# First layers and Haar attention of a one-core hybrid network kernel: steps regrouped over the engines

## The reference

```python
q = l2_normalize(apply_rope(x @ W_Q, cos, sin))      # rotation of two halves of 32
k = l2_normalize(apply_rope(x @ pinv(W_Q).T, cos, sin))
v = x @ W_V.T
attn_coef = (W_h.T q)(W_h.T k).T * scale             # W_h: Haar basis, constant over blocks of 32 tokens
attn = where(near, q k.T * scale, W_h attn_coef W_h.T)   # near only the own token with these masks
attn = attn / sqrt(number of visible tokens)          # causal
attn = softmax((attn - mean) / std) over visible tokens
y = attn @ v @ W_O.T
```

## Time and profile before

| | us |
|---|---|
| three runs | 367.94, 369.97, 475.1 |
| median of the three | 369.97 |
| profiled execution | 368.61 |
| its span, first to last instruction | 366.8 |
| of it: first layers, up to the attention's first steps | 0 to 45 |
| multi-head attention | 45 to 183.5 |
| first mixture and its layer norm | 183.5 to 231 |
| layer norm and Haar attention | 231 to 263.1 |
| layer norm, gate | 263.1 to 275.4 |
| second mixture | 275.4 to 366.8 |

### The profile page before, as it was taken

How to read it: one execution, slowest core, us unless ns; L and a number is a source line. 1 busy time by engine, 2 the same in 40 slices (tenths; PEclk the granted TensorE clock), 3 DMA queues, 4 the chain that set the end, 5 groups by cost and what they waited for, 6 DMA issues and landing times.

```text
span 366.8 us, 6880 instructions
## 1 busy us (share of the span) xinstructions
PE 333.8 (91%) x2287; PEld 214.7 (59%) x2296; DVE 265.8 (72%) x682; ACT 220.2 (60%) x557; POOL 164.0 (45%) x177
## 2 busy tenths in 40 slices
PE   8885669999999999999889999968698999999996
PEld 5652346777776777666464333524456776666661
DVE  2888898888889888887572786897986844445650
ACT  1554478889898888889539553542144643344550
POOL 6000057655556565555300000040200999999994
PEclk9998778999999999999989999988999999999999
DMA  7934000000000000000000992000003966656521
GB/s 214 249 110 152 0 1 0 3 3 1 2 0 3 3 0 2 2 2 0 2 3 8 334 386 82 2 1 0 2 2 113 348 194 217 209 199 207 173 81 58
DMA packets 16275, 30.86 MB, mean 84 GB/s; under 512 B 5808, under 2 KB 9584, under 8 KB 16240
## 3 DMA queue, kind: packets, MB, share of 16 engines
q1 hardware_dynamic: 15776, 29.60, 24.9%
q10 hardware_dynamic: 464, 0.82, 0.9%
HBM read 29.70 MB, written 0.72 MB: 83 GB/s over the span
## 4 chain that ended last, share of the span: by engine, by line
PE 68%; DVE 16%; ACT 8%; issue 4%; DMA 1%; POOL 1%; SPq 0%; DVEq 0%; ACTq 0%; POOLq 0%
PE ps L1148 15%; PE ps L1156 8%; PE ps L945 7%; PE ps L975 7%; PE ps L957 6%; PE ps L1096 5%; PE ps L1103 4%; ACT va_vb L674 2%; PE ps L923 2%; PE ps L869 2%; PE ps L1003 1%; PE ps L936 1%; DVE negmax L1746 1%; PE ps L1253 1%; DMA x<-in_x 1%
## 5 line engine op out<-in xcount | busy, mean ns | idle before, releaser
L534 POOL TENSOR_TENSOR va_vb<-va_vb,rowinv 128x512 f32<-128x512 f32 x63 | 65.5, 1040 | 53.6 <-DVE rowinv L1753 53.4
L674 ACT ACTIVATE va_vb<-ps,negmax 128x256 f32<-128x256 f32 x128 | 59.5, 470 | 10.8 <-DVE negmax L1746 10.0
L809 ACT ACTIVATE wy<-ps 128x512 f32<-128x512 f32 x64 | 38.1, 597 | 42.8 <-PE ps L1148 42.8
L1148 PE MATMUL ps<-XP,early 64*128 64x256 f32 x512 | 57.5, 379 | 0.0
L1148 PEld LDWEIGHTS ps<-XP,early 64*128 64x128 f32 x512 | 46.8, 186 | 12.4 <-issue 4.9
L945 PE MATMUL ps<-keys_gates,XX 128*128 128x512 f32 x128 | 47.6, 454 | 1.7 <-ACT va_vb L674 1.1
L957 PE MATMUL ps<-consts,va_vb 128*128 128x128 f32 x256 | 40.1, 280 | 5.1 <-POOL va_vb L534 2.8
L1746 DVE TENSOR_REDUCE negmax<-ps 128x2 f32<-128x512 f32 x64 | 43.9, 686 | 1.0
L957 PEld LDWEIGHTS ps<-consts,va_vb 128*128 128x128 f32 x256 | 30.1, 148 | 13.2 <-POOL va_vb L534 5.1
L975 PE MATMUL ps<-pT,vproj 128*64 128x256 f32 x256 | 35.7, 388 | 0.0
L665 ACT ACTIVATE keys_gates<-ps 64x256 fp32r<-64x256 f32 x64 | 24.2, 378 | 8.3 <-PE ps L923 7.1
(11 more groups left out here) (328 smaller groups left out, 636.6 us busy)
## 6 DMA issues: line engine op xcount, KB each, us to landing
pT<-gates_row SPq DMA_DIRECT2D x16, 512.0 KB, 4.8
vproj<-gates_row SPq DMA_DIRECT2D x14, 512.0 KB, 5.2
gate_row_keys<-gates_row SPq DMA_DIRECT2D x14, 512.0 KB, 5.1
early<-in_f_in SPq DMA_DIRECT2D x1, 2048.0 KB, 8.2
consts<-in_consts SPq DMA_DIRECT2D x1, 813.0 KB, 7.1
x<-in_x SPq DMA_DIRECT2D x1, 512.0 KB, 3.9
w2raw<-in_f_in SPq DMA_DIRECT2D x1, 512.0 KB, 6.0
out<-in_f_out SPq DMA_DIRECT2D x1, 512.0 KB
```

The costliest lines, as they stand in the source:

```text
L534: gp.tensor_tensor(prob[:, n % 4], prob[:, n % 4], rowinv[:, n % 4, :].unsqueeze(2).broadcast_to([P, U, N]), ALU.mult).then_inc(S("p_scale ...
L674: ins = act.activation(prob[:, n % 4, h, :], ps[:, 1 + n % 2, h * N:(h + 1) * N], ACT.Exp, bias=negmax[:, n % 4, h:h + 1], accum_out=rowsu ...
L809: act.activation(act_out[:, kk % 2, :].rearrange("p (o n) -> p o n", o=2), ps[:, 2 * pair_of(kk):2 * pair_of(kk) + 2, 0:2 * P], ACT.Silu). ...
L1148: mm = pe.matmul(ps[:, 2 * pair_of(kk) + o, w * 2 * P:(w + 1) * 2 * P], w3raw[r, e, w * HID:(w + 1) * HID], pairs(c, 2)[r], start=True, st ...
```

## The change

First layers. The two `gw` copies go from DVE to ACT, between the exponentials and the copy of `AA`. The sum over `w3n` goes ahead of the softmax maxima on DVE. The two given variances get their constant at DVE's start and their square root on ACT before the two `wy` copies, so that the square root for the joined variance is an instruction of its own. `x1` is made by one instruction per half from `wy` and the input, without the shift; the shift is added in the sign's bias and in the one-column terms. The ten one-column steps become five on two neighbouring columns. 8 unread products ahead of the convolution become 3.

Haar attention. `rotate` and `R` are gone: PE multiplies cosine parts and sine parts with the scaled basis and adds them in PSUM, 64 products on 16 columns in place of 32 on 8; the second half of the rotated columns is copied with its sign turned, and half of each result is not used. The products of the first half wait only for that half; norms, square root and inverse run by halves. The own-token product comes from the unrotated `QK` on POOL (two instructions of 512 columns). The copies of v are spread between ACT's other work; PE's block sums of v come after the spread of the coefficients, ACT copies their result out of PSUM and POOL masks it. The mask is added before the variance; maximum and subtraction stand beside the square root; the weights are normalised at the end. POOL makes two of the masked weight tables. For the second half of the tokens ACT scales v with `pdia` in 8 instructions of 64 columns and PE adds it in PSUM.

```diff
 @@ first layers, ACT
+            act.wait_ge(S("gw_done"), 1)
+            for g in range(G):
+                act.activation(gw[h, :, g, :], ps[h, 4, :]..., ACT.Copy).then_inc(S("gw_evac"), 1)
             act.wait_ge(S("folded"), 1)
...
+            act.wait_ge(S("bn_var_ready"), 1)
+            act.activation(col[:, 12:14], col[:, 9:11], ACT.Sqrt).then_inc(S("bn_std_ready"), 1)
             for p in range(2):
                 act.wait_ge(S("wy_counted"), p + 1)
...
-            act.activation(col[:, 11:14], col[:, 8:11], ACT.Sqrt)
-            act.activation(va[:, 512:1024], wy[:, 512:1024], ACT.Identity, scale=..., bias=...)
+            act.wait_ge(S("bn_var_ready"), 2)
+            act.activation(col[:, 11:12], col[:, 8:9], ACT.Sqrt).then_inc(S("bn_std_ready"), 1)
 @@ first layers, PE
-            keep_clock(pe, 2, 8)
+            keep_clock(pe, 2, 3)
 @@ first layers, DVE
+            ts(col[:, 9:11], v_both("v1"), EPS_BN, None, ALU.add).then_inc(S("bn_var_ready"), 1)
...
+            dve.wait_ge(S("l1_loaded"), 80)
+            dve.tensor_reduce(col[:, 20:21], w3n[:], AX.X, ALU.add, apply_absolute_value=True)
...
-                dve.tensor_copy(gw[h, :, g, :], ...).then_inc(S("gw_evac"), 1)
...
-                    step(ts(va[:, s], wy[:, s], col[:, 28:29], col[:, 29:30], ALU.mult, ALU.add))
-                tt(x1[:, s], va[:, s], x0[:, s], ALU.add).then_inc(S("x1_ready"), 1)
+                stt(x1[:, s], wy[:, s], col[:, 28:29], x0[:, s], ALU.mult, ALU.add).then_inc(S("x1_ready"), 1)
 @@ Haar, POOL
+            for half in range(2):
+                gp.tensor_tensor(same_token[:, q]..., QK[:, :, q, 0, :], QK[:, :, q, 1, :], ALU.mult)
+            gp.wait_ge(S("vsum_copied"), 1)
+            gp.tensor_tensor(vsum[:], vsum_all, con("sameb")..., ALU.mult).then_inc(S("vsum_evac"), 1)
+            gp.wait_ge(S("e9_ready"), 1)
+            gp.tensor_tensor(far_weights, e9[:, :, :, 0:NB], blocks("below"), ALU.mult)
+            gp.tensor_tensor(t9[:, :, :, 0:NB], e9[:, :, :, 0:NB], blocks("own"), ALU.mult)
...
-            for u in range(U):
-                gp.tensor_tensor(m_d[...u], V3[...u], pdia[...u], ALU.mult)
+            gp.tensor_tensor(m_d[...0], V3[...0], pdia[...0], ALU.mult).then_inc(S("diag_done"), 1)
 @@ Haar, ACT
+            values(0, 0)
+            for half in range(2):
                 act.wait_ge(S("qk_evac"), 2 * half + 2)
                 ... squares of the half
+            act.wait_ge(S("n2_ready"), 1)
+            ... square root of half 0; values(0, 1); square root of half 1; values(1, 0); values(1, 1)
...
             act.activation(F8[:], ps[0:NB, 1, 0:64], ACT.Copy).then_inc(S("F8_evac"), 1)
+            act.wait_ge(S("vsum_ready"), 1)
+            act.activation(vsum_all, ps[:, 3, :]..., ACT.Copy).then_inc(S("vsum_copied"), 1)
             act.wait_ge(S("a_var_ready"), 1)
...
             act.activation(p8T[:], ps[:, 5, 0:P], ACT.Copy).then_inc(S("p8T_evac"), 1)
+            for j in range(J):
+                for g in range(G):
+                    ins = act.activation(m_d[:, t*C:(t+1)*C], V3[:, t], ACT.Copy, scale=pdia[:, t:t+1])
 @@ Haar, PE
-            keep_clock(pe, 5, 8)
+            keep_clock(pe, 5, 10)
...
-                        for h in range(2):
-                            mm = pe.matmul(ps[h * C:(h + 1) * C, 0, ...], R[:, t, h], basis2[:, t, h], ...)
+                    for a, parts in enumerate(((m_a, m_b), (m_d, m_c))):
+                        for u in range(U):
+                            for k, part in enumerate(parts):
+                                mm = pe.matmul(ps[a * C:(a + 1) * C, 4, ...], part[:, t * C:(t + 1) * C],
+                                               basis2[:, t], start=(u == 0 and k == 0), stop=(u == 1 and k == 1))
...
             mm.then_inc(S("far_ready"), 1)
+            ... block sums of v (the four records of L1198), then_inc vsum_ready
...
+            pe.wait_ge(S("diag_last"), 1)
+            pe.matmul(ps[:, 1, :], ident, m_d[...1], start=False, stop=True).then_inc(S("yfar_ready"), 1)
             keep_clock(pe, 2, 8)
 @@ Haar, DVE
-            rotate(0); rotate(1); product and sum of R
+            norms(0); inverse_norms(0); basis_of(0); norms(1); inverse_norms(1); basis_of(1)
...
+            dve.tensor_copy(k8[...], low_rank(a, 1))                # twice
...
             ts(s9[:, 2], s9[:, 0], EPS_VAR, None, ALU.max).then_inc(S("a_var_ready"), 1)
+            step(dve.tensor_reduce(s9[:, 5], a9[:], AX.X, ALU.max))
+            step(tt(a9[:], a9[:], over(s9[:, 5]), ALU.subtract))
             dve.wait_ge(S("a_std_ready"), 1)
             step(dve.reciprocal(s9[:, 4], s9[:, 3]))
-            z9 times 1/std, plus mask, maximum, subtraction
+            tt(z9[:], a9[:], over(s9[:, 4]), ALU.mult).then_inc(S("z_ready"), 1)
...
+            tt(by_image(pown[:]), by_u(s9[:, 0]), by_u(s9[:, 7]), ALU.mult)
```

More of the change, by code:

```diff
@@ L497, in projected, with low_rank @@
             return ps[:, first + 2 * pair:first + 2 * pair + 2, 0:384].rearrange("p g (u c) -> p g u c", u=2)
+        def low_rank(a, which):
+            at = C * a + IC * which
+            return ps[at:at + IC, 4, 0:B * 2 * NB].rearrange("p (b h n) -> p b h n", h=2, n=NB)[:, :, which]
         def of_pair(a, half, pair):
@@ L1194, in l3_pe @@
             pe.wait_ge(S("v3_ready"), 1)
-            keep_clock(pe, 5, 8)
[L1196 to L1201, removed]
+            keep_clock(pe, 5, 10)
             for j in range(J):
                 if j % 2 == 0:
-                    pe.wait_ge(S("rotated"), j + 2)
+                    pe.wait_ge(S("cosines_done"), j + 2)
+                    pe.wait_ge(S("rope_pool"), j + 2)
                     pe.wait_ge(S("basis_ready"), j + 2)
@@ L1226, in l3_pe @@
             for u in range(U):
+                mm = pe.matmul(ps[:, 3, :], con("inblock")[:, u * P:(u + 1) * P],
+                               V3[:].rearrange("p (j u g) c -> p j u (g c)", j=J, u=U)[:, :, u, :],
+                               start=(u == 0), stop=(u == 1))
+            mm.then_inc(S("vsum_ready"), 1)
+            for u in range(U):
                 pe.matmul(ps[:, u, :], ident, T[:].rearrange("p (j u g) c -> p u j (g c)", j=J, u=U)[:, u],
@@ L1471, in blocks @@
-            def blocks(name):
-                return con(name).rearrange("p (u n) -> p u n", u=U).unsqueeze(2).broadcast_to([P, U, B, NB])
-            tt(p8[:], e9[:, :, :, 0:NB], blocks("below"), ALU.mult).then_inc(S("p8_ready"), 1)
-            step(tt(t9[:, :, :, 0:NB], e9[:, :, :, 0:NB], blocks("own"), ALU.mult))
-            for u in range(U):
-                ins = dve.tensor_reduce(of_u(pown[:], u), t9[:, u, :, 0:NB].rearrange("p (j g) n -> p j g n", g=G),
-                                        AX.X, ALU.add)
@@ new lines, in _, with half_of @@
+            tt(col[:, 34:36], inv, col[:, 22:24], ALU.mult)
+            step(tt(low, inv, v_both("m1"), ALU.mult))
+            step(tt(low, v_both("be1"), low, ALU.subtract))
+            step(tt(col[:, 36:38], low, v_both("b12"), ALU.add))
+            step(tt(col[:, 41:42], col[:, 36:37], shift, ALU.add))
+            def half_of(a, p):
+                return a[:, p * 512:(p + 1) * 512]
+            dve.wait_ge(S("x1_ready"), 2)
+            for p in range(2):
+                ins = ts(half_of(va, p), half_of(x1, p), col[:, 41:42], None, ALU.add)
@@ L1616, in norm_and_prelu @@
                     ALU.add).then_inc(S(done), 1)
-            for p in range(2):
-                ins = ts(half_of(va, p), half_of(x1, p), col[:, 36:37], None, ALU.add)
-            step(ins)
             for p in range(2):
```

219 lines of the change are left out of this document (107 added, 112 removed).

## The result

The changed kernel takes **371.59 us** (median of 9 runs, 370.44 to 373.59) against 369.97 for the kernel before in the same runs: **1.0068 times as long, 95% interval 1.0038 to 1.0098**, 2.5 us. The ratio is one of means and leaves out the one run of the kernel before that took 475.1 us, an execution in a slower state. The forecast was 367.0, with 371.0 as its upper end, on the scale of the profiled execution of 368.6; the profiled execution of the changed kernel took 371.79, its span is 370.0. The change is a small loss where a small gain was forecast.

What follows compares the result with a forecast made beforehand. The prediction took DVE's chain to bound the first layers, and PE's queue, then DVE and ACT alternating, the Haar attention. It summed 368.6 - 3.1 + 1.5 = 367.0 us, forecast 365 to 369, range 363.0 to 371.0.

Steps and rivals of the forecast that it cites:

- rival 2: Haar attention: small products become the stage's bound and the whole is slower, typical 371, at worst 373.9; chance 0.2.
- end of small products: Haar attention: the second half's products, on the path at half clock, end at 250.4 against 248.95, 1.4 us later.
- copies, coefficients, spread: Haar attention behind the small products: these steps keep their length.
- fused, variance: Haar attention behind the spread: two fused instructions save 0.1 us.
- root waits for the copy: Haar attention: the square root waits for ACT's copy of v's block sums, 0.1 to 2.0 us later, 1.2 taken.
- exponential: Haar attention, root to end of exponential: 2.2 us becomes 1.9, a gain counted as 0.35.
- to `p8`: Haar attention, exponential to `p8`: 1.62 us becomes 1.25; 0.2 counted as gain after a possible block by POOL.
- to `start_sums`: Haar attention, from `p8` to the sums: 5.6 us becomes 5.3 on PE, 0.4 counted as gained.
- Half clock: Haar attention: PE's clock expected at 0.5 for the second half's small products, 4.0 to 6.6 us, 4.2 taken.
- The price of a record: Haar small products: 32 ns in the old order, up to 19 ns more in the new, doubled by half clock.
- Blocking by POOL: Haar attention: DVE instructions on two SBUF operands stand still beside POOL, each losing up to 1.27 us, basis halves up to 2.5.
- Rival 3: First layers return only 1.3 us because the convolution runs at half clock, total 368.8; chance 0.1.

Runs made afterwards that it cites:

- the root-first run: The changed kernel with ScalarE's square root of the variance moved ahead of the copy of v's block sums; ratio to the kernel before 1.0090 [1.0055, 1.0125].
- the run with the first layers alone: The kernel before with only the new first layers, its Haar attention the old one; ratio to the kernel before 0.9958 [0.9934, 0.9983].
- the run with the new chain: The kernel before with new first layers and only the new Haar code behind the spread, old order of products; ratio 0.9919 [0.9886, 0.9952].

## Why the prediction was wrong

**The mechanism was rival 2**, small products as the bound of the stage, which had 0.2. On the forecast's scale they ended at 252.8, behind the 252.1 from which it said that the whole is slower, and the time came near its typical 371; its price of 51 ns a record at full clock did not show, it was 37. The forecast's sum of +1.5 in the Haar attention measured +5.1, its -3.1 in the first layers -1.9: 368.6 + 5.1 - 1.9 is the 371.8 of the profiled execution. Taken term by term from the two traces, each against the stage's start:

| step | forecast | measured |
|---|---|---|
| end of small products | +1.4 | +3.8 |
| copies, coefficients, spread | 0 | +0.5 |
| fused, variance | -0.1 | -0.1 |
| root waits for the copy | +1.2 | +1.8 |
| exponential | -0.35 | -0.4 |
| to `p8` | -0.2 | -0.3 |
| to `start_sums` | -0.4 | -0.2 |

**The failed step is the first one**: "The first half's products run before, hidden. The second half's 64 records stand on the path." That needed a basis at 243.1. On that scale it came at 245.3, because POOL stretched the addition and the basis pair by 2.6; by then the second basis was 2.3 away, less than the 3.9 that 64 records take at half clock, and all 128 ran in one go. The bound was in the text ("up to 2.5 for the two halves of the basis") but was put on the second half, where POOL was already through. The forecast's own numbers did not hide a half either: between its two bases lay 3.1 us, and a half at the half clock that it expected was 4.2; it priced the second half so and the first at nothing. With the block of the basis pair removed the stage is 1.6 shorter, with the clock kept through the products 2.5, with both edits 3.1.

**Half clock was foreseen, and its extent was not.** A fall behind the idle stretch stood in the forecast, but for one half of the products and with "the clock returning on the way". It stayed until 257.7, so the spread and the block sums paid as well: +0.5 and most of +1.8.

**The price of a record** came out near by luck. I took 4.2 for a half at half clock; 64 records at 61 ns are 3.9. Two errors nearly cancel: a record costs 37 ns at full clock and not 32, and half clock makes it 1.7 times as long and not twice. The 19 ns for runs in one column half, taken from the earlier trace rows, do not appear: 37 ns stand beside the 32 of the earlier trace rows, 5 more, with twice the columns. The rule quoted from the Trainium skill, "TensorE: Matmul & The Clock Gate", Part 3, by which the new order costs nothing, was nearer than the row of `start_sums`.

**The root's wait** came as forecast, 1.8 behind the variance, within the bounds of 0.1 to 2.0 and above the 1.2 taken. Whether it was on the path the root-first run could not show, as the table load stayed behind the copy.

**Blocking by POOL** was tied to "two SBUF operands". The trace shows it for an addition of a constant too (1.00 against 0.18), while the sum at 238.37 kept its 1.22 and the reciprocal at 240.90 its 0.25 beside a working POOL. The Trainium skill, "SBUF — State Buffer", Who interferes with whom, names `tensor_scalar` beside the operations with two inputs and exempts reductions; these rows agree.

**First layers.** The steps were right: convolution at 24.59 (forecast 24.3), the instruction of 29.86 at 26.84 (26.75), 3.0 earlier where 3.1 was forecast. Rival 3 did not come about: the clock is 1.0 through the convolution, from 24 to 29. What failed is that it was carried to the end undiminished. The lead was 2.6 at 31, 2.3 at 45 and 2.0 at 57, and the run with the first layers alone gained 1.5 [0.6, 2.4]. The first loss is the gap ahead of 30.95, for which the profile shows no wait. The second is a product that ran at a clock of 0.5 in the kernel after and of 1.0 in the kernel before (PE's timeline, after, then before):

```profile
42.72 0.77 PE L962 MATMUL ps<-XX,AA 128*128 128x256 f32 x2 [0.88 <-DVE XX L416]
...
45.31 0.47 PE L923 MATMUL ps<-XX,AA 128*128 128x256 f32 x2 [0.88 <-DVE XX L411]
```

That is this execution's: four other traces with the new first layers have 0.47 there. Of the third only the place is known, the next such product ahead of 57, and no run took the losses apart.

## What to carry to other kernels

Moving work off a busy VectorE can cost more than it saves when the engine behind it is TensorE in a stretch of waits: find first what keeps TensorE's clock up there, because every sum behind the fall pays, not only the products that were moved. An instruction given to GpSimd is priced by what VectorE has to do beside it, so put it where VectorE reduces or waits. When a change has separable parts, time them apart: here the first layers gained, the chain behind the spread gained 1.0 us in its trace, and with the new order of the products undone and TensorE kept at work the same kernel is 1.4% faster than before.

## What the runs showed of the hardware

- Small products with new weights each cost 37 ns a record at a clock of 1.0 (4.71 us for 128) and 61 at 0.5 (7.82): 1.7 times, while the block sums of 512 columns went from 1.72 (the chain of the run with the new chain, 242.06) to 3.71, about twice.
- PE counted as busy without a pause from 243.5 on, behind 3.8 us of idling, and the clock fell all the same at 244.1. With unread products up to 0.4 us before the start it held through the same 128 products and fell behind them, at 247.9. With 17 unread ones up to 0.5 us before the start it fell within them in one kernel (246.7); in another, traced twice, once between the halves (245.6) and once only behind them (250.3), during large fp32 products.
- VectorE's addition of a constant on 128x16 took 1.00 instead of 0.18 and a pair of products on 128x64 2.15 instead of 0.36 while GpSimd worked; a sum (1.22) and a reciprocal (0.25) kept their time.
- A table load is issued with the function that needs it, behind whatever stands ahead of that in ACT's order: moving the square root alone left the load 1.9 us behind it (254.46 to 256.37).
